# Last stage of a transformer layer with routed experts: VectorE adds every returned expert row, GpSimd makes the low parts of the shared expert's hidden rows

## What is computed

```python
probs = softmax(xf @ router_w); topw, topi = top_k(probs, 2)
h = silu(einsum('nd,edf->nef', xf, w1)); ye = einsum('nef,efd->ned', h, w2)     # 8 experts
routed = einsum('ne,ned->nd', combine, ye)
shared = sigmoid(xf @ shared_gate_w) * (silu(gate) * up @ shared_down)
out = h_residual + routed + shared
```

## Time and profile before

| what | value |
|---|---|
| median of 3 runs | 1049.62 us |
| the profiled execution's own time | 1047.3 us |
| its span in the profile | 1045.6 us |
| TensorE clock granted, whole span | 0.992 |
| last TensorE work of the experts ends | about 998.6 us |
| last add of VectorE ends | 1041.7 us |

### The profile page before, as it was taken

One profiled execution on the slowest core, in us unless ns is written; L12 is line 12 of the kernel. 1 busy time (PEld: TensorE's weight loads), 2 busy tenths in 40 slices (PEclk: granted clock), 3 DMA queues, 4 the chain that ended last, 5 costly groups with the idle time before them and its releaser, 6 DMA issues.

```text
span 1045.6 us, 23025 instructions
## 1 busy us (share of the span) xinstructions
PE 1002.3 (96%) x7978; PEld 866.4 (83%) x7978; DVE 735.2 (70%) x1896; ACT 653.0 (62%) x1923; POOL 510.6 (49%) x557
## 2 busy tenths in 40 slices
PE   7989999999999999999999999999999988999995
PEld 5867889888888888888888888889887887999974
DVE  3767775786788578768857876785784765666657
ACT  4658874786677478657847774784773644555521
POOL 0025543557356455735545573564445594444430
PEclk9999999999999999999999999999999999999998
DMA  7210000101100010110001011000114828444469
GB/s 258 85 47 2 2 2 1 42 1 42 41 2 22 22 41 2 42 42 2 21 22 41 2 42 41 2 17 27 41 36 181 290 58 278 134 133 134 133 196 316
DMA packets 42551, 74.29 MB, mean 71 GB/s; under 512 B 8152, under 2 KB 27384, under 8 KB 42440
## 3 DMA queue, kind: packets, MB, share of 16 engines
q1 hardware_dynamic: 35112, 52.89, 15.3%
q0 software_dynamic: 7056, 19.93, 5.7%
q10 hardware_dynamic: 272, 0.00, 0.0%
HBM read 40.28 MB, written 32.52 MB: 70 GB/s over the span
## 4 chain that ended last, share of the span: by engine, by line
PE 74%; DVE 9%; DMA 4%; ACT 3%; issue 2%; SPq 1%; POOL 0%; DVEq 0%; ACTq 0%; POOLq 0%
PE proj_ps L70 12%; PE proj_ps L72 12%; PE proj_ps L71 12%; PE proj_ps L777 10%; PE pT_ps L764 10%; PE s_ps L746 9%; DMA xg<-expert_in_rows 2%; ACT prob L1066 2%; PE s_ps L70 2%; PE s_ps L71 1%; PE s_ps L72 1%; PE s_ps L992 1%; DMA back<-expert_out_rows 1%; DVE z L1405 1%; PE pT_ps L1013 1%
## 5 line engine op out<-in xcount | busy, mean ns | idle before, releaser
L1066 ACT ACTIVATE prob<-s_ps,nmax 128x255 f32<-128x255 f32 x512 | 237.7, 478 | 140.1 <-DVE nmax L1278 139.3
L1719 POOL TENSOR_SCALAR prob<-prob,rinv 128x255 f32<-128x255 f32 x128 | 138.4, 1081 | 255.8 <-DVE rinv L1296 255.3
L1278 DVE TENSOR_REDUCE nmax<-s_ps 128x2 f32<-128x510 f32 x256 | 159.2, 679 | 23.2 <-PE s_ps L746 22.6
L764 PEld LDWEIGHTS pT_ps<-ident,prob 128*128 128x128 f32 x1024 | 114.6, 140 | 36.6 <-issue 28.3
L764 PE MATMUL pT_ps<-ident,prob 128*128 128x128 f32 x1024 | 136.7, 276 | 3.3 <-ACT probT L1092 3.1
L777 PE MATMUL proj_ps<-probT,v 128*64 128x256 f32 x1024 | 124.9, 386 | 0.0
L1721 POOL TENSOR_SCALAR prob<-prob,rinv 128x255 f32<-128x255 f32 x128 | 119.1, 931 | 0.0
L1285 DVE TENSOR_TENSOR qk_space<-proj_ps,qk_space 128x512 fp32r<-128x512 f32 x128 | 87.7, 685 | 35.2 <-ACT qk_space L1078 34.8
L1073 ACT ACTIVATE prob<-prob,rinv 128x255 f32<-128x255 f32 x128 | 67.2, 525 | 67.1 <-DVE rinv L1296 66.9
L746 PE MATMUL s_ps<-qk_space 64*128 64x256 f32 x1536 | 108.3, 287 | 0.4 <-DVE qk_space L1285 0.4
L1066 ACT ACTIVATION_READ_ACCUMULATOR prob<-s_ps,nmax 128x1 f32 x512 | 108.4, 212 | 0.0
(11 more groups left out here) (261 smaller groups left out, 2661.4 us busy)
## 6 DMA issues: line engine op xcount, KB each, us to landing
xg<-expert_in_rows SPq DMA_DIRECT2D x71, 130.0 KB
back<-expert_out_rows SPq DMA_DIRECT2D x6, 1024.0 KB, 18.8
xin<-in_x_dram SPq DMA_DIRECT2D x8, 512.0 KB, 4.1
z_columns<-z2T_hi SPq DMA_DIRECT2D x8, 512.0 KB, 2.6
z_columns<-z2T_lo SPq DMA_DIRECT2D x8, 512.0 KB, 3.6
z3T_hi<-z_columns SPq DMA_DIRECT2D x8, 512.0 KB, 6.7
z3T_lo<-z_columns SPq DMA_DIRECT2D x8, 512.0 KB, 7.4
out_dram<-resid SPq DMA_DIRECT2D x8, 448.0 KB
```

Of the source, the lines that this page charges most:

```text
L764: m = pe.transpose(pT_ps[h][:, o:o + P], prob[u_par(u)][:, h, qt, kt * P:(kt + 1) * P], ident[:])
L1066: m = act.activation(prob[u_par(u)][:, h, qt, 1:N], s_ps[b][h][:, qt * N + 1:(qt + 1) * N], ACT.Exp, bias=nmax[b][:, n:n + 1], accum_out=r ...
L1278: dve.tensor_reduce(nmax[b][:, 2 * h:2 * h + 2], s_ps[b][h][:].rearrange("p (q k) -> p q k", q=2)[:, :, 1:N], AX_X, ALU.max, negate=True). ...
L1719: pool.tensor_scalar(prob[k][:, 0, 1, 1:N], prob[k][:, 0, 1, 1:N], rinv[k][:, 1:2], None, ALU.mult).then_inc(s_nA1, 1)
```

## The change

`ADDED_BY_DMA` becomes 0: GpSimd's four accumulating transfers go, SP loads back all 8 groups, and VectorE adds them all. The low parts of groups 4 to 7 move from VectorE to GpSimd, which no longer waits for the scatters' landing. VectorE's order in the last stage is new. `EXPERTS_FIRST` becomes 4: `add_shared(g)` for g of 4 and above waits for `add_experts(g)`.

```diff
-        EXPERTS_FIRST = 7
+        EXPERTS_FIRST = SHARED_EARLY
-        ADDED_BY_DMA = 2
+        ADDED_BY_DMA = 0
...
             product(4, 0)
-            hidden_split_lo(4, 0)
             product(4, 1)
-            hidden_split_lo(4, 1)
             product(5, 0)
+            add_experts(0)
+            product(5, 1)
+            add_experts(1)
             add_experts(2)
-            hidden_split_lo(5, 0)
-            product(5, 1)
-            hidden_split_lo(5, 1)
+            product(6, 0)
             add_experts(3)
+            add_experts(4)
             add_shared(4)
-            product(6, 0)
-            hidden_split_lo(6, 0)
             product(6, 1)
-            add_experts(4)
-            hidden_split_lo(6, 1)
+            add_experts(5)
             add_shared(5)
             product(7, 0)
-            add_experts(5)
-            hidden_split_lo(7, 0)
+            add_experts(6)
             product(7, 1)
-            hidden_split_lo(7, 1)
+            add_experts(7)
             add_shared(6)
-            add_experts(6)
-            add_experts(7)
             add_shared(7)
...
-            def add_experts(g, k):
-                ...
-                pool.dma_start(resid[...], rows, accum_op=ALU.add).then_inc(s_back[g], 16)
-            for k in range(SLOTS):
-                pool.wait_ge(s_yst[k], 16 * len(range(k, RUN, SLOTS)))
-            for k in range(TOP):
-                for g in range(ADDED_BY_DMA):
-                    add_experts(g, k)
+            for g in range(SHARED_EARLY, GROUPS):
+                hidden_split_lo(g)
```

## The result

The changed kernel takes **1055.99 us** (median of 7 executions, 1050.81 to 1058.92); the kernel before, timed beside it, 1049.28. The ratio is 1.006, with a 95% interval of 1.0033 to 1.0088: slower, as forecast, but by 6.3 us by this ratio (6.7 between the medians) instead of 2.7, and above the range.

The account below looks back on a forecast made before the run. VectorE, hardly ever free behind a late load, was taken to bound the last stage. Order 1.9 us earlier and holds of 4.7 gave 2.7 us later: 1049.62 + 2.7 = 1052.3 us, range 1047.4 to 1054.3.

Parts of the forecast that it names:

- The hold: Last stage: a GpSimd low part falling inside a pair's first add delays VectorE's second add, taken as 0.95 us.
- The sum of the holds, 4.7: Last stage: 0.6 us for adds 0, 4.6 for five others, less a used-up pause of 0.5, gives 4.7.
- the likeliest case: VectorE's adds in the last stage: holds of 0.6 to 1.27 us, chance 0.62, own range 1050.2 to 1054.2 us.
- rival 1: GpSimd and VectorE in the last stage: no hold or one under 0.49 us, time 1047.7 us; chance 0.28.
- The 0.6 for the first pair: Adds 0 on VectorE start at 1009.2 after low part (5,0), ready at 1008.3; delay 0.6 us.
- The order, free of charge and at full clock: VectorE's new last-stage order, with GpSimd's low parts costing nothing, ends at 1039.8, 1.9 us earlier.
- Loads "2.5 to 2.9": The last stage's loads of `back` land 2.5 to 2.9 us apart and stay hidden.
- rival 2: Last-stage loads land 3.8 us apart because loads and earlier stores fill the DMA engines; time 1052.1 us; chance 0.10.
- the walk: VectorE's last-stage items timed one behind another; without a charge for GpSimd the last adds end at 1039.8.
- The tail, 3.87: After VectorE's last add only the last group's stores remain, 3.87 us, kept as before.
- Its rows of group 5 start 1.0 us behind shared 4: TensorE before product (7,0): group 5's rows start 1.0 us behind shared 4 and take 2.8 us.
- The predicted pause of 0.5 us ahead of product (7,0): VectorE waits 0.5 us for TensorE before product (7,0) in the walk without holds; holds use the pause up.

Follow-up runs that it names:

- lo_stub: The changed kernel with GpSimd's eight subtractions cut to one column each, so the low parts are mostly left out; ratio 0.9998 to the kernel before.
- lo_memset: The changed kernel with GpSimd writing zeros over its eight low-part tiles instead of subtracting, so it reads nothing; ratio 1.0021 to the kernel before.
- warm_full: The changed kernel with 30 and 12 unread matmuls filling TensorE's pauses ahead of the shared rows of groups 5 and 7; ratio 1.0041.
- stub_warm: The changed kernel with one-column low parts on GpSimd and 18 and 6 unread matmuls in TensorE's pauses ahead of groups 5 and 7; ratio 0.9978.
- after_again: The changed kernel itself, unchanged, run for a second profile and more executions; median 1056.12 us, ratio 1.0066 to the kernel before.
- lo_twice: The changed kernel with each GpSimd subtraction made twice and 34 and 16 unread matmuls in TensorE's pauses; 1053.19 us in one execution, no ratio.
- after_order: The changed kernel with VectorE's 16 adds placed one by one among products and shared rows; ratio 1.0029 to the kernel before.
- warm: The changed kernel with 22 and 10 unread matmuls in TensorE's pauses ahead of the shared rows of groups 5 and 7; ratio 1.0049.

## Why the prediction was wrong

**Right, by its own steps.**
- The hold. "It lasts to the end ... I take 0.95 us": measured 0.95 to 0.98 (2.17 to 2.20 against 1.22), in the six second adds named and not in the two others. The first was taken at 0.6 and cost the same as the rest. The rule of the Trainium skill weighed there ("SBUF — State Buffer", section "Who interferes with whom") names the right pair of instructions. The block for a whole instruction, which the section states of VectorE's two-port modes and the prediction applied to these adds, would be 1.27, and the second add lost 0.97. lo_stub shows the cause by cutting the reading down to a column, and lo_memset beside it that it is reads and not writes.
- The sum of the holds, 4.7: 5.2 between warm_full and stub_warm. This was the likeliest case, and rival 1 (no hold) is dead. The 0.6 for the first pair failed because its load came earlier, so that the low part fell inside the add and not ahead of it.
- The order, free of charge and at full clock: 1.9 us earlier predicted, 2.6 in stub_warm. The 0.7 between them is the earlier first load, which the walk didn't count on.
- Loads "2.5 to 2.9": 2.55 from the second on, and rival 2 is dead. "Hidden" holds only in part: the second came 3.4 us behind the first, and without the hold VectorE waits for it, 0.91 us in lo_stub, 0.21 in lo_memset and not at all in stub_warm. The first add came 6.66 us after the first product, taken as 7.17; that is luck, and it made the forecast look better by 0.5.
- The tail, 3.87: 3.85. VectorE's work, unchanged but for the holds.

**The step that failed** is in the walk: "Its rows of group 5 start 1.0 us behind shared 4 ... and take 2.8 (to 1022.87)". The start is right (1024.11 behind 1023.09). The 2.8 us are those of a TensorE at full clock, read where it had waited 2.09 us. By the walk's own numbers TensorE had nothing to do from the end of its matmuls for product (6,1) (1018.0, as in the trace before) until about 1022.9, some 4.9 us, and the holds made it 7.42. The clock fell to 0.50 and the rows took 5.2 us. The holds aren't needed for it: in lo_stub the wait is 5.55 and the rows take 4.9. The predicted pause of 0.5 us ahead of product (7,0), "used up" by the holds, was 1.91 us instead. Against warm_full that makes 2.3 us of stage in one profile and, with the fall in group 7's rows, 3.3 in the other, 0.3 of each being the first load.

| us of stage, against before | predicted | measured |
|---|---|---|
| order alone | -1.93 | -2.61 (stub_warm), 0.7 of it the first load |
| holds | +4.7 | +5.16 (warm_full less stub_warm) |
| clock, with 0.3 of first load | 0 | +2.25 (after less warm_full), +3.25 (after_again) |
| sum | +2.77 | +4.80, +5.80 |

The range took its upper end from the size of a hold alone. With a fall of the clock as a case of its own it would have reached some 3 us higher.

**What stays open.** The medians moved by 6.3 and 6.9 us (0.6% and 0.66% of 1049), the stages by 4.8 and 5.8. warm_full is 4.3 us over by its ratio and 2.6 by its stage. These gaps of 1 to 2 us lie within the intervals, which are 1.8 to 2.9 us to either side, and profiles of single executions, whose stage begins anywhere between 1000.2 and 1006.5, can't close them. Why it begins there was not tried. How often the second fall comes in executions without a profile is not known either.

## What to carry to other kernels

Work moved to an idle GpSimd is not free where VectorE at that moment adds two SBUF tiles: each low part of 0.6 us taken off VectorE cost it 0.97 us. Here six of eight were charged: 5.8 us for 4.8 saved. When an order is walked through on paper, write down TensorE's idle stretches too, and price what follows a long one at both clocks. And before shortening an engine's line, look at what drains behind it: with the stores held back by the accumulating transfers, 2.8 us off VectorE's line met a tail 1.4 us longer and medians that didn't move.

## What was not expected of the hardware

- GpSimd and VectorE alternated, instruction by instruction, when both had reads of SBUF queued (lo_twice: 2.07 and 2.30 us for subtractions of 1.28, 1.72 to 2.31 for adds of 1.22). The TENSOR_SCALAR of the earlier trace rows, another kind of operation, came through only behind two GpSimd operations in a row.
- The length of TensorE's wait alone didn't settle whether the clock fell. It was at 1.00 through waits of 3.00 us (before) and 3.44 (after, ahead of group 7's rows), and fell around waits of 4.14 (after_order) and 7.42 (after), but also around one of 2.37 (warm), where one of 2.32 (lo_twice) had none. The same wait of 3.44 us ahead of group 7's rows had no fall in after and one in after_again.
- After the fall in the kernel after, the clock came back 5 us into group 5's rows (1024.11 to 1029), so the whole of this batch of 24 matmuls was paid at half speed.
